# Five instruction streams of one Trainium2 core merged by a new table of numbers: the order of issue alone is other

## The reference

```python
h = _layernorm(x) * (1 + ca) + sa
x = x + ga * _L0_attn_ref(h, ...)
h = _layernorm(x) * (1 + cb) + sb
x = x + gb * _L0_ffn_ref(h, ...)
```

```python
z = xn @ W_in
gate = jax.nn.silu(xn @ W_gate)
dt = jnp.clip(jax.nn.softplus(z @ W_dt + b_dt), 0.001, 1.0)
h = exp(dt * A) * h + dt * B * z
y = (h * C).sum(states) * gate
```

## Time and profile before

| | |
|---|---|
| three runs | 3286.68, 3280.89, 3285.47 us, median 3285.47 |
| span of the profiled execution | 3287.9 us, which is 2.4 us over the median; no time outside of the span is given for it |
| mean granted TensorE clock | 0.940 |
| busy: PE, DVE, ACT, POOL | 88%, 83%, 64%, 59% |
| matmuls, DVE, ACT, POOL instructions | 14848, 4612, 3852, 1541 |
| HBM read and written | 288.27 MB and 17.35 MB |
| period of chunks 0, 1, and 2 to 14, first scan to first scan | 170.4, 176.9, and 188.2 to 190.4 us |
| after the last scan (tail) | 246.4 us |

### The profile page before, as it was taken

The page is one execution under the profiler, slowest core; times in us unless marked ns, Lnnn a source line. Parts: engine busy times, 40 slices in busy tenths (PEclk is TensorE's granted clock), DMA queues, the critical chain, the costliest instruction groups (busy, mean ns, idle before and its releaser), DMA issues.

```text
span 3287.9 us, 45422 instructions
## 1 busy us (share of the span) xinstructions
PE 2907.9 (88%) x14848; PEld 2380.8 (72%) x14848; DVE 2739.3 (83%) x4612; ACT 2096.2 (64%) x3852; POOL 1925.7 (59%) x1541
## 2 busy tenths in 40 slices
PE   6567698998999899898989989899999989998898
PEld 4455477787877778687777868777777877777676
DVE  3777989797998979799898979889897989989541
ACT  2546476676757677675767767576766767575433
POOL 1766667564766757475675756576575647666110
PEclk8558699999999999999999999999999999999998
DMA  4241123231322323232322323232232323223122
GB/s 130 96 159 39 52 81 111 92 102 64 129 82 91 125 78 100 70 118 85 100 103 81 106 79 125 66 106 92 87 109 86 108 76 121 78 71 120 56 103 76
DMA packets 152778, 308.56 MB, mean 94 GB/s; under 512 B 18368, under 2 KB 96984, under 8 KB 135136
## 3 DMA queue, kind: packets, MB, share of 16 engines
q1 hardware_dynamic: 152000, 302.52, 27.6%
q10 hardware_dynamic: 272, 1.57, 0.1%
q0 software_dynamic: 272, 1.57, 0.1%
HBM read 288.27 MB, written 17.35 MB: 93 GB/s over the span
## 4 chain that ended last, share of the span: by engine, by line
PE 48%; DVE 18%; issue 13%; ACT 12%; POOL 5%; DMA 1%; DVEq 0%; SPq 0%; POOLq 0%; ACTq 0%
PE ps_B L1870 11%; PE ps_B L1765 10%; PE ps_A L1765 8%; DVE hs L1527 8%; PE ps_H L1760 7%; DVE acc L1491 5%; PE ps_H L1778 4%; PE ps_B L1760 3%; POOL bu L1100 3%; PE ps_B L1778 3%; PE ps_B L1917 2%; ACT ps_A L1288 2%; DMA bb<-b_rows 1%; DVE hA L1719 1%; ACT acc L1300 1%
## 5 line engine op out<-in xcount | busy, mean ns | idle before, releaser
L1100 POOL TENSOR_TENSOR bu<-z,bb 128x512 f32<-128x512 f32 x1024 | 1294.2, 1290 | 289.9 <-DVE hs L1527 146.7
L1527 DVE TENSOR_TENSOR_SCAN hs<-ps_A,state,bu 128x512 f32<-128x512 f32 x768 | 976.5, 1276 | 21.7 <-ACT ps_A L1288 11.4
L1288 ACT ACTIVATE ps_A<-dt,a_neg 128x512 f32<-128x512 f32 x1024 | 699.3, 686 | 355.7 <-DVE hs L1527 351.5
L1760 PE MATMUL ps_H<-ident,hs 128*128 128x128 f32 x4096 | 652.6, 294 | 195.3 <-DVE acc L1491 123.1
L1760 PEld LDWEIGHTS ps_H<-ident,hs 128*128 128x128 f32 x4096 | 528.3, 151 | 329.2 <-DVE acc L1491 152.0
L1870 PE MATMUL ps_B<-ws_out,hid 128*128 128x256 f32 x2944 | 699.4, 382 | 15.5 <-ACT hid L1437 6.1
L1491 DVE SCALAR_TENSOR_TENSOR acc<-ps_H,ctok,acc 128x512 f32<-128x512 f32 x960 | 700.2, 731 | 8.0 <-PE ps_H L1760 7.1
L1870 PEld LDWEIGHTS ps_B<-ws_out,hid 128*128 128x128 f32 x2944 | 537.0, 191 | 85.1 <-ACT hid L1437 9.9
L1765 PE MATMUL ps_B<-fh,ws_in 128*128 128x512 f32 x1440 | 537.6, 418 | 10.3 <-DVE bl L1680 4.3
L1527 DVE TENSOR_TENSOR_SCAN hs<-ps_A,bu 128x512 f32<-128x512 f32 x256 | 310.9, 1216 | 32.2 <-ACT ps_A L1288 20.0
L1765 PEld LDWEIGHTS ps_B<-fh,ws_in 128*128 128x128 f32 x1440 | 271.0, 188 | 70.5 <-DVE cb L1664 8.1
(11 more groups left out here) (349 smaller groups left out, 4807.7 us busy)
## 6 DMA issues: line engine op xcount, KB each, us to landing
ws_in<-w_split SPq DMA_DIRECT2D x126, 1024.0 KB, 5.4
bb<-b_rows SPq DMA_DIRECT2D x256, 256.0 KB, 3.9
ws_out<-in_L_ffn_V_rwkv SPq DMA_DIRECT2D x64, 512.0 KB, 5.8
ws_out<-in_L_ffn_W SPq DMA_DIRECT2D x32, 512.0 KB, 6.9
xb<-in_L_attn_x SPq DMA_DIRECT2D x16, 512.0 KB, 5.3
n<-in_L_attn_x SPq DMA_DIRECT2D x16, 512.0 KB, 3.9
w_split<-wsp SPq DMA_DIRECT2D x8, 1024.0 KB, 5.6
out<-xb SPq DMA_DIRECT2D x16, 512.0 KB, 3.2
```

What stands on the lines that cost most here:

```text
L1100: pool.tensor_tensor(bu[:, u % 4, :], z[:, d, :], bb[:, s % 2, :], ALU.mult)\
L1288: act.activation(b.t[:, :], dt[:, d, :], ACT.Exp, scale=a_neg[:, d, s:s + 1])\
L1527: dve.tensor_tensor_scan(hs[:, s % 2, d, :], b.t[:, :], bu[:, k % 4, :], state[:, s, d:d + 1] if i % CPB else 0.0, ALU.mult, ALU.add)\
L1760: return pe.transpose(dst, src, ident[:, :])
```

## The change

Only the table `PACE` is other, in all five engines' parts. No operation, buffer, wait or semaphore is other, and the order within a lane is the same; which pieces stand before which unit changes. The table takes four lines less, so line numbers behind it are lower by 4 in the rows of the change below (L983 is L979, L930 is L926, L1209 is L1205, L1288 is L1284). It was made anew with the waits of VectorE and GpSimd for each other at their shared port to SBUF counted. The first lines of the diff, and two that the text below speaks of:

```diff
     "sp": {
-        "w_fold": 3, "w_in0": 15, "w_in1": 26, "w_out0": 36, "w_in2": 38, "w_out1": 48, "w_in3": 49, "w_out2":
...
-        217, "sw": 229, "e0_0": 232, "e0_1": 241, "e0_0_down": 242, "e0_1_down": 250, "e1_0": 253, "e1_0_down":
...
+        "w_fold": -2, "w_in0": 9, "w_in1": 41, "w_out0": 41, "w_in2": 42, "w_out1": 67, "w_in3": 78, "w_out2": 80,
...
+        92, "ffn_1": 95, "ffn_0_down": 102, "ffn_1_down": 125, "end_mod_f": 94, "end_ffn_0": 94, "end_ffn_1": 95,
+        "end_ffn_0_down": 95, "end_ffn_1_down": 128, "mod_x": 118, "rv": 209, "sw": 230, "e0_0": 250, "e0_1": 250,
+        "e0_0_down": 250, "e0_1_down": 250, "e1_0": 250, "e1_0_down": 258, "e1_1": 264, "e1_1_down": 265, "out": 281,
```

More of the change, by code:

```diff
@@ L168 @@
     "sp": {
[6 rows of a table removed]
-        253, "e1_1": 265, "e1_1_down": 267, "out": 286, "last_mod_x": -26, "last_rv": 161, "last_sw": 172,
-        "last_e0_0": 204, "last_e0_1": 209, "last_e0_0_down": 221, "last_e0_1_down": 232, "last_e1_0": 240,
-        "last_e1_0_down": 277, "last_e1_1": 346, "last_e1_1_down": 346, "last_out": 348,
[8 rows of a table added]
+        "last_out": 343,
     },
     "pool": {
[3 rows of a table removed]
-        152, "rstd_e": 164, "h2": 190, "x_bias": 191, "rstd_h": 214, "rstd_i": 219, "rstd_j": 220, "rstd_m":
-        238, "x5": 286, "last_rstd_e": 169, "last_h2": 170, "last_x_bias": 172, "last_rstd_h": 179,
-        "last_rstd_i": 181, "last_rstd_j": 186, "last_rstd_m": 192, "last_x5": 260,
+        "w_low0": 40, "w_low1": 53, "w_low2": 77, "w_low3": 91, "w_low4": 91, "w_low5": 94, "w_low6": 105, "w_low7":
+        110, "mean0": -45, "rstd0": -39, "h0": -27, "mean1": -18, "rstd1": -16, "gx": 17, "u0": 17, "u1": 17, "u2":
+        27, "u3": 27, "xg": 42, "rstd_a": 96, "x_prob": 147, "end_rstd_a": 102, "end_x_prob": 127, "rstd_e": 180,
+        "h2": 187, "x_bias": 197, "rstd_h": 200, "rstd_i": 200, "rstd_j": 209, "rstd_m": 238, "x5": 289,
+        "last_rstd_e": 149, "last_h2": 151, "last_x_bias": 151, "last_rstd_h": 170, "last_rstd_i": 180, "last_rstd_j":
+        183, "last_rstd_m": 194, "last_x5": 259,
     },
     "act": {
[21 rows of a table removed]
[20 rows of a table added]
     },
     "dve": {
[5 rows of a table removed]
-        201, "ao1": 204, "h_stats": 204, "h_norm": 206, "i_stats": 208, "i_norm": 208, "j_stats": 209, "lowx0":
[4 rows of a table removed]
-        164, "last_ao1": 165, "last_h_stats": 165, "last_h_norm": 165, "last_i_stats": 173, "last_i_norm": 173,
[4 rows of a table removed]
[14 rows of a table added]
     },
     "pe": {
[27 rows of a table removed]
[25 rows of a table added]
     },
```

## The result

The changed kernel takes 3295.74 us (median of 7 runs, 3294.47 to 3298.01). The kernel before took 3286.68 us beside it (7 runs, 3280.89 to 3287.61). The ratio is 1.003 with a 95% interval of 1.0021 to 1.004, so the change makes the kernel slower by 0.3%, 9 us. The profiled execution spans 3293.2 us, 5.3 us more than that of before; that of before, 3287.9 us, lies above all seven of its timed runs, so the traces show less of the difference than the medians do.

A forecast was written before the change was run, and what follows sets the result against it. DVE's scan and readout were taken to bound the scans and PE the seam. The terms summed to +0.6 us on a profiled span of 3287.9, thus 3288.5, or 3286 us for the median; range 3269 to 3302.

The forecast's parts named there:

- rival 2: Slower, 3301 us: e0_0 comes late on PE, DVE waits 1.3 us in each of 14 chunks; chance 0.21.
- E: X weight loads on SP bunched behind bb 8: e0_0 lands about when PE needs it, +2.8 us (0 to +18).
- What bounds the kernel: DVE's scan and readout set the scans, PE the seam; better order could win about 50 us in 1024 scans.
- B: ACT's e_norm behind the exp of unit 62: 0.3 us more into each seam, +4.2 us (0 to +9.8).
- D: ffn_1_down's load on SP ahead of bb 2: POOL may hand the delay on, +2.8 us (0 to +0.4 x 14).
- A: Loads of bb 7 and 8 on SP ahead of e0_0 and e0_1: scans' waits for bu gone, -3.5 us (0 to -3.5).
- The table would have next to nothing to win in the scans: Scan and readout escape contention with POOL at the SBUF port; the prize, 10.4 us and as many again, lies in the seam.
- C: PE's transposes of unit 56 ahead of p5: half of DVE's readout wait there goes, -1.6 us (0 to -3.2).
- F: Smaller moves that fill gaps: -2 us in the seam (0 to -2.8) and -1.3 us in the tail.
- G: Chunk 0: w_prod makes DVE wait 2.9 us, most bb stalls go; together -0.8 us (-4.1 to +3.8).
- Rival 1: Faster, 3276 us: SP's late loads land in time, E and D are 0 and B costs half; chance 0.30.
- What would show it: Signs in the changed profile, such as unit 62's wait gone and periods of chunks 2 to 14 moving at most 0.7 us.

The follow-up runs named there:

- a_e00: The changed kernel with SP issuing e0_0 after unit 12 again, not after unit 30: 3277.02 us, 0.9969 of the kernel before.
- e0_0: Not a run: a 1 MB load of X weights issued by SP, first read by PE's o0_up; after unit 12 in the kernel before, after unit 30 in the changed one.
- e0_1: Not a run: the other 1 MB load of X weights issued by SP, 33 us after e0_0 in the kernel before, together with it in the changed one.
- a_c: The changed kernel with ACT issuing c2 behind unit 1 again: 3295.37 us.
- a_three: The changed kernel with the numbers of a_e00 and a_c undone, and e_norm on ACT ahead of the exp of unit 62 again: 3270.04 us.
- b_bb: The kernel before with SP issuing e0_1 and e0_0_down after unit 27, behind bb 7, and e0_0 where it was: 3305.76 us.
- b_bb_xprob: b_bb with POOL issuing x_prob after unit 25, as in the changed table: 3285.74 us.
- a_four: a_three with SP issuing ffn_1_down behind unit 17 again: 3260.97 us.
- a_xprob: a_four with POOL issuing x_prob after unit 25, not after unit 24: 3276.86 us.
- a_wprod: a_four with w_prod on PE ahead of the transposes again in chunk 0: 3260.87 us.

## Why the prediction was right or wrong

The range (3269 to 3302) held the time, and the chance of slower was given as 0.3. The likeliest case, no measurable change at 3286, was wrong: the kernel is slower by 9 us, 0.28%, and the bound was 0.2%. By its own last sign it was wrong as a whole too: the periods of chunks 2 to 14 moved by -0.6 to +2.8 us, +1.0 in the mean, where 0.7 was the limit. What happened is rival 2 with more won elsewhere than it allowed. That the miss is no larger than 9 us is in part luck: E alone was 16 us too low, and gains that the sum did not have covered part of it.

- **What bounds the kernel**: right for the scans. What was found is idle time of DVE there, the start of `e_norm` on the way into the seam, and one busy time that I did not look for. For the end of the seam it was incomplete, see the section on the hardware.
- **E, the bunched loads**: this term failed. I took +0.2 us per chunk between 0 and 1.3, 2.8 us in all, and it was 1.3, 18.7 us in all by a_e00. The step that failed is "lands 5.4 us later": 5.4 is the median over the loads of before, where `e0_0` went out alone (4.7 to 5.6 us), and in the change `e0_0` and `e0_1` and both `_down` loads go out within 3 us. They share what one had, and 7.3 to 7.8 us came of it for the first. Rival 2 had this mechanism, its price (1.3 x 14) and its decision point (over 5.9 us). I let the median of the row decide against it. Its sentence from the Trainium skill, page "SBUF — State Buffer", section "Summary: rules for kernel authors", about 358 GB/s for HBM to SBUF, gave the last of the 3.1 MB at 8.8 us and so spoke for the middle of that range. The trace shows 395 GB/s on average from 1255.7 to 1260.6, more than the page says, and still the first load was late: it lands first, but with the others in flight beside it. The last lands 12.6 us after the first is issued, since the issues alone take 3.4 us and the rate is 88 to 99 GB/s at first. The second way in which E could cost, bb 9 late for unit 36, did not come: no scan of unit 36 waits.
- **B, e_norm**: right in place and size. +4.2 forecast, -4.6 us when undone; 0.38 us per chunk by the rows and not 0.3.
- **D, ffn_1_down**: right in place. +2.8 forecast; in the changed kernel the waits at unit 8 are 1 us more than the 2.9 of before. They are 4 us more once c2 is moved (a_c, a_three), and hardly more with e0_0 early alone (4.6 us in a_e00). Undoing the move there gave 9.1 us, of which the waits show 4.1.
- **Not in the sum**: c2 ahead of unit 1 on ACT, a new wait of 0.67 to 0.73 us in each chunk, which cost nothing by a_c.
- **A, bb 7 and 8**: the waits of the scans went as forecast. POOL's wait for bb fell from 133.2 us (32 waits; the loads are those of the second row) to the second number here (us, times):

```profile
  DVE hs L1523: 303.0, 373
  DMA bb<-b_rows: 37.4, 21
```

  But alone it would have cost 20 us, by b_bb, of which 14 are shown to come through the port; and with `x_prob` moved as well (b_bb_xprob) it is worth 0.5 us and not 3.5. I had said that POOL's wait is worth 3.5 us, and had not asked whom it shields.
- **"The table would have next to nothing to win in the scans"**: this is the reasoning error of the text. I read the contention off the router's rows in the seam, where DVE has slack, and took scan and readout as all of DVE's work in the scans. `choice` has products of two SBUF inputs too. They showed 0.17 us before only because POOL stood on a late load. Against the kernel before the table wins nothing there (0.16 us after), but without its new position of `x_prob` a_four is 15.9 us slower (a_xprob). And "all of it where DVE is idle" was wrong for the seam's end, see the section on the hardware.
- **C, F**: the wait at unit 56 is gone in all 14 chunks, so the full -3.2 and not half. Against before a_four also gains 0.2 to 0.45 us near unit 24, and its scans of chunks 4, 8 and 12 are 2.1 to 3.1 us shorter in all, which I had not in the sum. In the traces a_four is 30 us shorter: 5 in chunk 0, 19 in chunks 1 to 14, and 6 in chunk 15 with the tail. These gains were not tried one by one.
- **G, chunk 0**: -0.8 forecast, -5.4 in the traces. The bb stalls went as forecast; `w_prod` made DVE wait 1.07 us and not 2.9, and by a_wprod nothing of it counts. The W chain behind it cost nothing.
- **Rival 1** is the case without E and D and with B at half. The nearest version tried, a_four, has none of the three and also c2 undone, and takes 3261 us, so the rival's 3276 left out 15 us of gains.
- **What would show it** said that E fails "if the idle time before PE's L1765 or L1870 names a DMA". It was there, 1.04 to 1.59 us in each chunk, and named "issue" in 13 of 14. The sign was right and its wording would have missed it.

## What to carry to other kernels

A load that is moved next to another one must be priced with both in flight, not with the median of loads that went alone; here the first of two large ones, with two smaller ones behind, took 7.3 to 7.8 us where it had taken 4.7 to 5.6 alone. Before an idle time of one engine is taken away, ask what it keeps free for the others: a wait of POOL here hid 1 us per chunk of contention at the port that it shares with DVE, and one bu more or less in front of a tiny DVE product was worth 16 to 20 us. A table of numbers made anew as a whole can hold large gains and a few dear mistakes at once, so undo its boldest moves one by one before judging it: here four numbers of several hundred turned 9 us lost into 25 won, and one of the four, c2, was worth nothing measurable alone.

## What the runs showed of the hardware that was not expected

- A DVE product of 128x12 elements took up to 1.22 us against 0.16, behind a bu of POOL that takes 1.28. A small instruction pays for the whole rest of the large one, and its row shows as busy and not as idle, so that no view of waits has it. At L1591, the subtraction that makes `fl`, the changed kernel has more of this than the one before: 62.0 us for 60 instructions against 46.3.
- One of these is the last thing that DVE does before a chunk's first scan. In the changed kernel, chunk 5, and then in the kernel before, chunk 6, where the blocked row is the router's product ahead of `fl`:

```profile
1007.89 1.80 DVE L1591 TENSOR_TENSOR fl<-ff,fh 128x512 fp32r<-128x512 f32 x1
1009.62 1.27 DVE L1523 TENSOR_TENSOR_SCAN hs<-ps_A,state,bu 128x512 f32<-128x512 f32 x1
```

```profile
1200.89 0.86 DVE L1569 TENSOR_TENSOR prob<-lg_m,lg 128x4 f32<-128x4 f32 x1
1201.67 0.68 DVE L1595 TENSOR_TENSOR fl<-ff,fh 128x512 fp32r<-128x512 f32 x1
```

  POOL's product `z*dt` ends at 1009.15 in the first and at 1201.72 in the second. The exp that the first scan needs is ready 0.60 to 0.62 us before that scan starts in the changed kernel, and 0.67 to 0.69 us in the kernel before, in chunks 2 to 15; in chunk 1, where DVE stands idle in front of the scan, it is 0.13 to 0.14 us. So contention at the port seems to cost both kernels an estimated 0.5 us at the end of each seam, 7 us in all (0.60 - 0.13, over 14 chunks). No run here moves these rows apart, so this is read off the traces and not shown.
- The clock: after 5.9 us of idle time on PE, a granted clock of 0.50 for 10.2 us goes with a stretch 1.1 us longer than the 59.2 us, and one for 6.8 us with nothing, although PE is busy nearly all of that stretch. In the two seams where the 6.8 us lay 3 to 4 us later the stretch took 61.4 us.
- The seam's two lengths, which alternated from chunk to chunk in the kernel before (59.1 to 59.4 and 60.3 to 60.7 in most chunks), go with the clock: within one kernel the order of the work is the same in both. A difference of 1 us per chunk between two kernels can be of this kind. What decides in which chunk the clock is back sooner was not found.
